# Hard-tile search and layer norms of a two-step graph kernel, rearranged on one core

## The reference

```python
def _top_p_attention(X, W1, W2, W3):
    q = X @ W1.T @ W2.T
    k = X @ W3.T
    probs = softmax(q @ k.T)
    # keep_sorted = cs - sp < 0.9, by probability, largest first
    A = probs * mask
    return A / A.sum(-1)

R = (S + eye) / (S + eye).sum(-1)
for n in range(2):
    A = _top_p_attention(Xa, W1, W2, W3)
    Xf, Xa = R @ Xf, A @ Xa
    Z = Z + Xf @ U1[n].T + Xa @ U2[n].T
h = X + Z
y = (h - mean(h)) / sqrt(var(h) + 1e-5) * ln_g + ln_b
out = layernorm(x + y)
```

## Time and profile before

| | us |
|---|---|
| median of 3 runs (1875.42 to 1879.34) | 1876.28 |
| the profiled execution | 1873.67 |
| its span, first to last instruction | 1872.0 |

### The profile page before, as it was taken

The page is one execution under the profiler, slowest core; times in us unless marked ns, Lnnn a source line. Parts: engine busy times, 40 slices in busy tenths (PEclk is TensorE's granted clock), DMA queues, the critical chain, the costliest instruction groups (busy, mean ns, idle before and its releaser), DMA issues. The chain is left out here.

```text
span 1872.0 us, 18415 instructions
## 1 busy us (share of the span) xinstructions
PE 1550.3 (83%) x4817; PEld 897.4 (48%) x4817; DVE 1400.4 (75%) x3789; ACT 762.9 (41%) x1182; POOL 247.3 (13%) x264
## 2 busy tenths in 40 slices
PE   6999999931799999999999999941179677867995
PEld 3555555521455555554666665631145343434553
DVE  4777777739477777767999999961879799798564
ACT  3444444421356565655444444421133332323332
POOL 1011111123000000000011111012010421221224
...
GB/s 239 200 183 199 183 181 182 175 1 0 103 200 198 185 185 192 206 208 198 179 172 181 179 179 180 179 3 3 1 3 1 7 1 6 7 6 1 7 6 12
DMA packets 55436, 211.89 MB, mean 113 GB/s; under 512 B 24832, under 2 KB 33600, under 8 KB 34736
## 3 DMA queue, kind: packets, MB, share of 16 engines
...
...
## 5 line engine op out<-in xcount | busy, mean ns | idle before, releaser
L1512 DVE MAX8 cand<-psL 128x8 f32<-128x256 f32 (+1 forms) x640 | 372.3, 583 | 95.7 <-PE psL L776 92.2
L1105 ACT ACTIVATE psL<-psL,umax 128x1024 f32<-128x1024 f32 x256 | 278.6, 1088 | 333.5 <-DVE umax L1506 329.5
L775 PE MATMUL psL<-kA,mq 128*128 128x512 f32 x512 | 298.7, 583 | 8.0 <-DVE mq L1339 7.6
L1234 ACT ACTIVATE ebuf<-psL 128x1024 f32<-128x1024 f32 x128 | 131.0, 1023 | 303.1 <-PE psL L952 254.9
L753 PE MATMUL psO<-adj_in,xn 128*128 128x512 f32 x512 | 241.1, 595 | 0.0
L894 PE MATMUL psO<-ebuf,xn 128*128 128x512 f32 x512 | 241.1, 593 | 0.0
L753 PE MATMUL psO<-adj_in,xf 128*128 128x512 f32 x512 | 240.7, 594 | 0.1
L1773 DVE SCALAR_TENSOR_TENSOR ebuf<-ebuf 128x1024 f32<-128x1024 f32 x128 | 156.7, 1224 | 99.6 <-PE psO L894 93.1
L776 PE MATMUL psL<-kB,mq 66*128 66x512 f32 x512 | 203.6, 398 | 0.0
L1171 ACT ACTIVATE ebuf<-psL 128x1024 f32<-128x1024 f32 x128 | 131.0, 1023 | 136.4 <-PE psL L866 136.4
L951 PE MATMUL psL<-mq,kA 128*128 128x512 f32 x256 | 151.7, 593 | 41.1 <-DVEq L1968 41.1
...
## 6 DMA issues: line engine op xcount, KB each, us to landing
adj_in<-in_adjT SPq DMA_DIRECT2D x128, 1024.0 KB, 4.8
...
list_dram<-ids,place POOLq DMA_INDIRECT x64
rel_prob<-cut_dram SPq DMA_DIRECT2D x32, 2.0 KB
cut_dram<-ncut SPq DMA_DIRECT2D x16, 2.0 KB, 8.8
```

The costliest lines, as they stand in the source:

```text
L775: nc.tensor.matmul(o, qA[:, t * P:(t + 1) * P], kA[:, c:c + BI], start=True, stop=False)
L1105: nc.scalar.activation(ps[:], ps[:], ACT.Exp, bias=umax[:, bass.ds(i * UB + k, 1)], scale=1.0, accum_out=usum[:, bass.ds(i * UB + k, 1)]). ...
L1234: nc.scalar.activation(raw_unit(n), psL[w % 3][:], ACT.Exp).then_inc(g["slot_read"], 1)
L1512: last = v.max(cand[:, t % 2, at + c * 8:at + c * 8 + 8], psL[(turn + k) % 3][:, c * WIDE:(c + 1) * WIDE])
```

## The change

**The search.** The threshold is a root squared times the top: the root starts at 0.5 and moves by halves (`next_try`), so no powers are taken, and `tile_factors`, `tile_bounds` and their waits go. `chord` interpolates in the root. 40 values are sorted, in five rounds, not 48. Where a flag is set, the bisection begins at its first step instead of its fifth. The steps get consecutive numbers n and a table of units; the first five steps of a tile are run at the end of the pair of blocks before (`BEFORE`).

**The layer norms.** VectorE takes mean and variance of each row by `bn_stats` and `bn_aggr` (`spread`), GpSimd the factor and the offset (`spread_of`), ScalarE centres and scales in one pass (`centre`, at u 10 and 15), and GpSimd adds gain, shift and x (`add_rows`).

**The order.** `z_add` at u 7, `spread` at u 8, the second at 13; `mix_q_lo` and `cut_rows` at u 11 with the query's matmul at u 10; the tile's rows at u 8, its query at 9, its logits from 10; the flag at u 3, `tile_cut` at 4, `mix_last` at 5. The features' gather has a semaphore of its own.

**Ranking of step two.** x is added to the other terms by GpSimd (`add_x`), not by an identity matmul. The last block's terms come after the tally on TensorE and before the first tile on VectorE. `ref_dram` is laid out like the norms. After the sweep ScalarE centres the last block before it copies the last tile's rows.

```diff
-    NEXT = 48
-    BIAS = 0.12
+    NEXT = 40
+    BIAS = 10.0
...
-    PREP_ROWS, PREP_Q, PREP_LOGITS = 7, 8, 11
+    PREP_ROWS, PREP_Q, PREP_LOGITS = 8, 9, 10
...
-        rest_in = ebuf[:, 0:N // UNIT, :].rearrange("p a b -> p (a b)").rearrange("p (e c) -> p c e", c=N // CHUNK)
+        rest_in = ebuf[:, 0:N // UNIT, :].rearrange("p a b -> p (a b)").rearrange("p (k c e) -> p c k e", k=8, c=N // CHUNK)
...
-                            sp.dma_start(ref_dram[bass.ds(i * BI, BI), :].rearrange("(t p) o -> p (t o)", p=P),
+                            sp.dma_start(ref_dram.rearrange("(p t) o -> p (t o)", p=P)[:, rows],
...
+                def add_x(i, h):
+
+                    pool.wait_ge(g["r_zo_sb"], 2 * i + h + 1)
+                    pool.sem_inc(met, 1)
+                    rows = slice(i * TB + h * ZT, i * TB + (h + 1) * ZT)
+                    nc.gpsimd.tensor_tensor(t2[:, 0:ZT, :], t2[:, 0:ZT, :], xn[:, rows, :], ALU.add).then_inc(g["r_zx_sb"], 1)
+
                 assert JQ == TB and PARTS == NB
                 add_self(0)
                 for i in range(NB):
-                    if i < NB - 1:
+                    if i < RING - 1:
                         add_self(i + 1)
+                    if s > 0:
+                        add_x(i, 0)
+                    if RING - 1 <= i < NB - 1:
+                        add_self(i + 1)
+                    if s > 0:
+                        add_x(i, 1)
                     pool.wait_ge(g["st_place"], i + 1)
...
-                        for dst, src, at in ((xgs[:, st, :], source, 0), (hrefs[:, st:st + 1], ref_dram, 0),
-                                             (htops[:, st:st + 1], top_dram[s], 1)):
-                            if src is ref_dram:
-                                pool.wait_ge(g["cut_out"], 64 * NB)
+                        nc.gpsimd.indirect_dma_start(
+                            out=xgs[:, st, :], out_offset=None, in_=source,
+                            in_offset=bass.IndirectOffsetOnAxis(ap=gids[:, st, 0:1], axis=0),
+                            bounds_check=N - 1, oob_is_err=False).then_inc(g["h_x"], 16)
+                        pool.wait_ge(g["cut_out"], 64 * NB)
+                        for dst, src in ((hrefs, ref_dram), (htops, top_dram[s])):
                             nc.gpsimd.indirect_dma_start(
-                                out=dst, out_offset=None, in_=src,
-                                in_offset=bass.IndirectOffsetOnAxis(ap=gids[:, st, at:at + 1], axis=0),
-                                bounds_check=N - 1, oob_is_err=False).then_inc(g["h_x"], 16)
-
-                    def tile_factors(r, c):
-
-                        pool.wait_ge(g["h_ratio"], r * PT + c + 1)
-                        nc.gpsimd.tensor_tensor(hmove[:].rearrange("p a k -> p (a k)"),
-                                                hratio[:].to_broadcast([P, 2 * (FIRST + 1)]),
-                                                hexponent[:].rearrange("p a k -> p (a k)"), ALU.pow).then_inc(g["h_move"], 1)
+                                out=dst[:, st:st + 1], out_offset=None, in_=src,
+                                in_offset=bass.IndirectOffsetOnAxis(ap=gids[:, st, 1:2], axis=0),
+                                bounds_check=N - 1, oob_is_err=False).then_inc(g["h_ref"], 16)
...
-                    def scaled(r, i, ln):
+                    def spread_of(r, i, ln):
 
                         pool.wait_ge(g["var_sb"], r * (NB * 2) + i * 2 + ln + 1)
                         chained(nc.gpsimd.tensor_tensor(rstd[:], var[:], power[:], ALU.pow))
-                        last = nc.gpsimd.tensor_tensor(t1[:], t1[:], rstd[:].unsqueeze(2).to_broadcast([P, TB, D]), ALU.mult)
-                        if ln == 0:
-                            chained(last)
-                            chained(nc.gpsimd.tensor_tensor(t1[:], t1[:], gain[:].unsqueeze(1).to_broadcast([P, TB, D]), ALU.mult))
-                            chained(nc.gpsimd.tensor_tensor(t1[:], t1[:], shift[:].unsqueeze(1).to_broadcast([P, TB, D]), ALU.add))
-                            nc.gpsimd.tensor_tensor(t1[:], t1[:], xn[:, i * TB:(i + 1) * TB, :], ALU.add).then_inc(g["normed"], 1)
-                        else:
-                            last.then_inc(g["res_sb"], 1)
+                        nc.gpsimd.tensor_tensor(offset[:], nmean[:], rstd[:], ALU.mult).then_inc(g["rstd_sb"], 1)
+
+                    def add_rows(r, i):
+
+                        pool.wait_ge(g["centred"], r * NB + i + 1)
+                        pool.sem_inc(met, 1)
+                        chained(nc.gpsimd.tensor_tensor(t1[:], t1[:], gain[:].unsqueeze(1).to_broadcast([P, TB, D]), ALU.mult))
+                        chained(nc.gpsimd.tensor_tensor(t1[:], t1[:], shift[:].unsqueeze(1).to_broadcast([P, TB, D]), ALU.add))
+                        nc.gpsimd.tensor_tensor(t1[:], t1[:], xn[:, i * TB:(i + 1) * TB, :], ALU.add).then_inc(g["normed"], 1)
+
+                    def scaled(r, i):
+
+                        spread_of(r, i, 0)
+                        add_rows(r, i)
+                        spread_of(r, i, 1)
...
-                        nc.tensor.matmul(psT[:, 2 * e + 1, :], xaT[:, c:c + P], u_sb[:, 1, 0, :], start=True, stop=False)
-                        last = nc.tensor.matmul(psT[:, 2 * e + 1, :], ident[:], xn[:, i * TB + t, :], start=False, stop=True)
+                        last = nc.tensor.matmul(psT[:, 2 * e + 1, :], xaT[:, c:c + P], u_sb[:, 1, 0, :], start=True, stop=True)
...
+                ranks(NB - 1)
+                pe.wait_ge(g["st_tally"], NB)
                 if s == 0:
                     to_rows(NB - 1)
-                    pe.wait_ge(g["r_n_sb"], NB)
                 else:
                     z_terms(NB - 1, 0)
                     z_terms(NB - 1, 1)
-                    pe.wait_ge(g["r_z_sb"], 2 * NB)
-                ranks(NB - 1)
...
+                            if u == 3 and i % 2 == 1 and p < PT:
+                                tile_flag(r, p + 1)
...
-                            if u == 10 and i % 2 == 1 and p < PT:
-                                pe.wait_ge(g["m_z_add"], r * NB + i)
-                                tile_flag(r, p + 1)
-                            if u == 12 and i < NB - 1:
+                            if u == 10 and i < NB - 1:
...
+                    def centre(r, i, ln):
+
+                        act.wait_ge(g["rstd_sb"], r * (NB * 2) + i * 2 + ln + 1)
+                        if ln == 0:
+                            act.wait_ge(stored, r * (NB * 16) + i * 16 + 16)
+                        for t in range(TB):
+                            last = nc.scalar.activation(t1[:, t, :], (yn if ln == 0 else t1)[:, t, :], ACT.Identity,
+                                                        bias=offset[:, t:t + 1], scale=rstd[:, t:t + 1])
+                        last.then_inc(g["centred"] if ln == 0 else g["res_sb"], 1)
...
                         mix_o_copy(r, NB - 1)
+                        centre(r, NB - 1, 0)
+                        centre(r, NB - 1, 1)
                         tile_rows_copy(r, PT + 1)
...
+                    def next_try(k):
+
+                        link(v.tensor_scalar(hstep[:], hsums[:, k:k + 1], htarget[:], 2.0 ** -k, ALU.is_ge, ALU.mult))
+                        link(v.scalar_tensor_tensor(out=hroot[:], in0=hstep[:], scalar=-(2.0 ** -(k + 1)), in1=hroot[:],
+                                                    op0=ALU.add, op1=ALU.add))
+                        link(v.scalar_tensor_tensor(out=htry[:], in0=hroot[:], scalar=hupper[:], in1=hroot[:],
+                                                    op0=ALU.mult, op1=ALU.mult))
...
+                    def chord():
+
+                        v.scalar_tensor_tensor(out=hparts[:], in0=hsums[:], scalar=htarget[:], in1=hsums[:],
+                                               op0=ALU.is_lt, op1=ALU.mult)
+                        link(v.tensor_scalar(hroot[:], hroot[:], 2.0 ** -(FIRST + 1), None, ALU.add))
+                        v.tensor_reduce(hbelow[:], hparts[:], AX.X, ALU.max)
+                        link(v.tensor_scalar(hspread[:], hsums[:], htarget[:], -LOWEST, ALU.is_lt, ALU.mult))
+                        v.scalar_tensor_tensor(out=hend[:], in0=hroot[:], scalar=hupper[:], in1=hroot[:],
+                                               op0=ALU.mult, op1=ALU.mult)
+                        link(v.tensor_tensor(hspread[:], hspread[:], hsums[:], ALU.max))
+                        link(v.tensor_reduce(hover[:], hspread[:], AX.X, ALU.min))
+                        v.tensor_tensor(habove[:], htarget[:], hbelow[:], ALU.subtract)
                         link(v.tensor_tensor(hover[:], hover[:], hbelow[:], ALU.subtract))
                         link(v.reciprocal(hover[:], hover[:]))
...
+                        link(v.scalar_tensor_tensor(out=habove[:], in0=hend[:], scalar=-BIAS, in1=habove[:],
+                                                    op0=ALU.mult, op1=ALU.add))
```

(58 more changed lines are left out.)

243 lines of the change are left out of this document (96 added, 147 removed).

## The result

The changed kernel takes 1803.86 us (median of four runs, 1802.05 to 1805.14), the kernel before 1877.81 on the same chips; the ratio is 0.9601, with an interval of 0.9575 to 0.9626. Forecast were 1811.8. The profiled execution took 1805.14 around a span of 1803.5, where that of before has 1872.0: 68.5 us less by the spans, where the terms of the forecast sum to 64.5.

What follows compares the result with a forecast made beforehand. The prediction saw a chain of stages ended by different engines: TensorE in ranking, VectorE late in the sweep's three search pairs. Its terms sum to -64.5 us, giving 1811.8 from the median of 1876.28; range 1793 to 1835.

Steps and rivals of the forecast that it cites:

- Step one's hard tile: Step one's search: no power, maxima over runs of 32, one sort round fewer, shorter chord; -4.8 us.
- Ranking of step two: Step two's ranking blocks: identity matmul goes, GpSimd adds x; -4 us, between -6.2 and +3.
- End of that ranking: Last logits to first gather: z terms after the tally -3.8, later scatters, shorter landing; -7.2 us in all.
- the landing: Wait for step two's list scatters to land before the gather: 4.67 us, as in step one, instead of 14.87.
- Gather and first tile: Gather to the sweep's first logits: earlier transposition -2.5, bounds without power -2.0, search -0.5; -5.0 us.
- The sweep: Four pairs of blocks: cheaper norms, flag and cut rows earlier, search steps moved; -42 us, between -25 and -52.
- the moved steps: Sweep: five search steps of the next tile, 14.7 us, run a pair earlier; pair 0 gains them, pair 2 only gives.
- "Nothing": Sweep: ScalarE's eight added centring instructions a block, about 1.1 us for four, cost nothing because ScalarE is mostly idle.
- Tail: After the sweep: norms 3.2 us shorter, centring before the last tile's rows; -1.5 us, between -5 and +3.
- The search never missed its bracket: Rival on the hard tiles' search: flagged rows force bisection, 119 us more, 1931 us; chance 0.04.
- "The sweep stays bound": Rival: ScalarE's stops for GpSimd cancel the norms' gain (+16) and cost seven blocks 1.5 each; about 1838 us; chance 0.10.
- "The ranking pays": Rival in step two's ranking: GpSimd's additions hold VectorE up and the landing stays 14.87; 1834 us; chance 0.05.

Runs made afterwards that it cites:

- x_by_identity: Changed kernel with x added by an identity matmul on TensorE again, GpSimd adding nothing; 1805.3 us.
- before_ref: Kernel before with only the reference stored in runs of four, in the layout of the norms, and gathered by it; 1860.25 us, ratio 0.9928.
- The square: Four kernels, old or new norms and sweep order; sweeps: both old 481.1 us, new norms only 442.2, new order only 453.0, both new 440.8.
- query_late: Changed kernel with the next block's query where it was before, matmul at unit 12, cut rows at 14 or 15; 1829.2 us.
- steps_home: Changed kernel with all 19 search steps of a tile in its own pair of blocks, none run ahead; 1813.3 us.
- three_edits: Changed kernel with early last list scatters, centring at units 11 and 3, and the last tile's preparation between the tail's two centrings; 1796.7 us.

## Why the prediction was right, and where it wasn't

*Step one's hard tile.* Right term by term: the sums start 2.0 sooner (1.8 forecast), four halvings cost 0.55 more (0.6), the chord 0.25 less (0.4), the maxima 5.33 in place of 7.94 (2.6 less for 2.5), a sort round 0.7.

*Ranking of step two.* -6.4 for -4. The price of the identity matmul was exact, 0.89 a block for 0.88, and x_by_identity gives it back. The 2.2 that were held back (4 for at most 6.2) were not needed for GpSimd's hand-over. Block 0 is 1.0 longer (45.5 for 44.5), but it takes 45.5 in x_by_identity too, where GpSimd adds nothing; why is open. 1.1 of the rest are the unexplained stops of before.

*End of that ranking.* -14.8 for -7.2, the largest miss. Of it 5.9 are the unexplained stop, which the forecast took for a part of the kernel: without it the tally comes 3.8 sooner, to the tenth what was forecast for z's terms. The scatters' delay behind the tally was 7.4, where 6.6 were forecast (9.0 from tally to scatter for 2.4). The step that was mis-sized is the landing: 4.67 was taken from step one, where the scatters follow the tally at once, and measured were 2.30. With the scatters early again the wait is 5.83 (before_ref) and 6.07 (x_by_identity): 4.67 was too little for early scatters and too much for late ones. Of the 7.4 us of delay 3.8 would have been waited for the landing anyway.

*Gather and first tile.* -3.9 for -5.0, in two parts. Up to the copy of the flags the stage is 5.8 shorter; TensorE's transposition came 5.9 after the gather for 8.1, 2.1 of the 2.5 forecast. Behind the copy it is 1.9 longer. There VectorE's next instruction past the branch stands 3.96 us, for 1.52 before (the changed kernel, then the kernel before):

```profile
1325.03 0.16 DVE L1971 RECIPROCAL hkept<-hkept 128x1 f32<-128x1 f32 x1 [3.96 <-remote]
```

```profile
1354.57 0.16 DVE L1953 RECIPROCAL hkept<-hkept 128x1 f32<-128x1 f32 x1 [1.52 <-DVE hflags L1935]
```

The forecast has no term for this stop, and every profile of the changed code has it (3.8 to 4.0). The tile's cut goes out behind this point, and the cut rows for the first logits wait 4.22 us more, until a DMA lands, so the 2.4 us by which the stop is longer lie on the path, as the order of these rows reads.

*The sweep.* -37.3 for -42: the size was near, the division was wrong. The price of a new norm was right, 1.59 on VectorE for 1.6, and its saving nearly, 1.50 for 1.6. The threshold's instructions lost their meetings, the product of `hrun` falling from 1297 ns to 200, but the norms alone or the order alone suffice for that. The failed step is the sum: 4 for the flag and 5.3 for the cut rows were added per pair to 6.4 for the norms. The square shows that they don't add: the order's 28.1 beside old norms is 1.4 beside new ones, and 18.1 of the 28.1 is idle time of VectorE that the order takes away beside old norms alone. The norms alone lower TensorE's wait for the flag from 30.2 to 13.8 with the flag unmoved, yet VectorE's idle time by only 4.1: a shorter wait of TensorE is not as much less idle time of VectorE. What the norms give, they give as work. That TensorE's waits and VectorE's stops behind them are VectorE's lateness seen from two sides, so that whatever makes VectorE less late shortens both, fits the square but is not shown; query_late, 24.9 of idle time with the work unchanged, shows that lateness of one piece in the queue counts beside the sum of the work.

That the total still fitted is luck in part, since a second error lay on the other side: the moved steps were priced by pairs, at a net loss of 7.5 (14.7 in pair 0, 7.2 back in pair 2), where steps_home shows them to gain 9.4. The forecast had also missed the 9.4 us stop for the prepared tile's query in block 0, which now holds 16 of the 19 steps. In its own sum the -15.1 for pair 0 is not -18.9 less one block's norms of 3.2, which makes -15.7.

*ScalarE and GpSimd.* "Nothing" was forecast for the centring, with stops behind GpSimd as a rival. The stops came (40.3 us in 11), with exponentials behind them, which the forecast had named as a sign of being wrong. three_edits priced them: VectorE felt 6.1, and was busy for 5.3 more when they were taken away, 4.7 of it in the two instructions of the cut rows, beside GpSimd's passes. Four centrings took 1.65 for the forecast 1.1. The stops were long in part because GpSimd's power, 1.01 alone, can stand behind VectorE's instructions. Of the fourteen in the sweep two, started 0.17 us after a sum of 2.35, took 3.06 and 3.05; two took 1.02 beside maxima, which have one input. The first two lines are one beside a sum and one beside maxima, the last one alone:

```profile
1455.44 3.06 POOL L644 TENSOR_TENSOR rstd<-var,power 128x4 f32<-128x4 f32 x1 [8.33 <-DVE var L2007]
...
1517.95 1.02 POOL L644 TENSOR_TENSOR rstd<-var,power 128x4 f32<-128x4 f32 x1 [10.26 <-DVE var L2007]
...
1780.22 1.01 POOL L644 TENSOR_TENSOR rstd<-var,power 128x4 f32<-128x4 f32 x1 [10.58 <-DVE var L2007]
```

The forecast had read the meetings as a partial loss of 0.6 to 1.1. A product that takes 200 ns alone took 1297 beside passes of 1.29, and the power can take three times its own length. That reads as one waiting for the rest of the other, and the small losses as late arrivals, not as a share. The rule that was weighed ahead (the Trainium skill, SBUF — State Buffer, section SBUF: two separate sides, that the two exclude one another for the whole instruction) describes these rows better than the forecast's reading did. Its price, three passes of 1.3 a block, didn't come either: in the sweep as changed the passes met mostly the cut rows (1130 ns for 744) and no sum (2345 ns, for 2344 with three edits). The rule gives the most that a meeting can cost, and the place of the instructions decides how many there are.

*The other rule*, on the fixed cost of small instructions (the Trainium skill, VectorE: DVE Perf Modes, section The TRN2 errata — SBUF-src ops pay a fixed extra latency per instruction), gave an estimate of 0.78 for four statistics; the trace has 0.86 to 0.87.

*Tail.* -1.0 for -1.5, and by the mechanism that was forecast: GpSimd's drain would have ended at 1798.8, but the last tile's preparation, now behind both centrings, ended at 1803.

*Rivals.* The search never missed its bracket; no bisection line appears. "The sweep stays bound" named the stops rightly and was wrong in its price (16 for the norms): at most 6 us of it were there, and taking the stops away did not give them back. "The ranking pays" did not come. Of the other signs, the ranking blocks took 46.4 for 46.7, and the gather came 3.3 us after the start of the last scatter for about 5.
